# An attention and FFN kernel on one core: the values of pairs 4 to 15 from seven block products in place of eight

## The reference, cut to what matters

```python
D, HEADS, HEAD = 512, 32, 128                  # x is 2 batches x 512 tokens x 512
x = hidden_states
h = layernorm(x)
q = rms_norm(h @ Wq + bq, gq)                  # over all 32*128 columns
k = rms_norm(h @ Wk + bk, gk)
v = h @ Wv + bv
a = softmax(q_head @ k_head.T / sqrt(128))     # per batch and head
o = concat_heads(a @ v_head) @ Wo + bo
x = x + layernorm(o)
x = x + layernorm(ffn(layernorm(x)))           # 512x512 base, 8 gated experts of rank 16
```

## Time and profile before

| | |
|---|---|
| time, median of 3 runs | 1073.78 us (1073.11 to 1077.03) |
| profiled execution, first to last instruction (span) | 1069.7 us |
| the profiled execution's own time | not listed apart; the median of the runs lies 4.1 us above the span |
| TensorE busy | 1052.9 us (98%) |
| VectorE, ScalarE, GpSimd busy | 789.6 (74%), 741.3 (69%), 681.1 us (64%) |
| TensorE's granted clock, mean | 0.998 of full speed |

### The profile page before, as it was taken

How to read it: one execution, slowest core, us unless ns; L and a number is a source line. 1 busy time by engine, 2 the same in 40 slices (tenths; PEclk the granted TensorE clock), 3 DMA queues, 4 the chain that set the end, 5 groups by cost and what they waited for, 6 DMA issues and landing times.

```text
span 1069.7 us, 20038 instructions
## 1 busy us (share of the span) xinstructions
PE 1052.9 (98%) x5781; PEld 563.7 (53%) x5781; DVE 789.6 (74%) x1831; ACT 741.3 (69%) x1470; POOL 681.1 (64%) x597
## 2 busy tenths in 40 slices
PE   7999999999999999999999999999999999999997
PEld 4444444444445655555555555555555555555454
DVE  8767766666645887777777777777777777778887
ACT  4666766666656787676777767677776767777756
POOL 2667767676657476676666667666666766666713
PEclk9999999999999999999999999999999999999999
DMA  6688985656663679977676776767677676765702
GB/s 240 175 237 261 269 232 194 223 215 222 203 142 135 199 187 267 227 173 177 177 184 165 189 179 165 176 178 187 162 190 179 163 176 180 189 163 128 175 33 79
DMA packets 312072, 197.76 MB, mean 185 GB/s; under 512 B 275424, under 2 KB 279392, under 8 KB 312032
## 3 DMA queue, kind: packets, MB, share of 16 engines
q1 hardware_dynamic: 304400, 193.71, 65.5%
q10 hardware_dynamic: 7632, 3.57, 1.5%
HBM read 94.45 MB, written 35.68 MB: 122 GB/s over the span
## 4 chain that ended last, share of the span: by engine, by line
PE 91%; DVE 5%; ACT 2%; DMA 1%; issue 1%; SPq 0%; POOL 0%; DVEq 0%; ACTq 0%
PE ps L1236 30%; PE ps L1237 30%; PE ps L1238 30%; DMA wa_stage<-w_qk 1%; DVE pair_q L2061 1%; ACT ps L1031 0%; DVE ps L2047 0%; DVE stats L1630 0%; DMA pair_k<-pair_q 0%; ACT xh L1024 0%; ACT pair_q L1040 0%; PE ps L1348 0%; DVE y L2011 0%; DVE wa_lo L1735 0%; DVE y L2172 0%
## 5 line engine op out<-in xcount | busy, mean ns | idle before, releaser
L2047 DVE TENSOR_SCALAR_CACHE_REDUCE ps<-ps,score_down 128x512 f32<-128x512 f32 x256 | 177.5, 756 | 88.6 <-PE ps L1238 87.9
L2061 DVE SCALAR_TENSOR_TENSOR pair_q<-ps,row_inv,pair_q 128x512 f16<-128x512 f32 x256 | 174.5, 744 | 54.7 <-ACT pair_q L1040 54.6
L1031 ACT ACTIVATE ps<-ps,neg_max 128x512 f32<-128x512 f32 x256 | 168.2, 657 | 44.9 <-DVE ps L2047 44.9
L1236 PE MATMUL ps<-xh,wa_hi 128*128 128x512 f16 x512 | 194.3, 379 | 1.8 <-DVE wa_lo L1735 1.8
L1237 PE MATMUL ps<-xl,wa_hi 128*128 128x512 f16 x512 | 194.3, 379 | 0.0
L1238 PE MATMUL ps<-xh,wa_lo 128*128 128x512 f16 x512 | 194.3, 379 | 0.0
L1040 ACT ACTIVATE pair_q<-ps,row_inv 128x512 f16<-128x512 f32 x256 | 154.9, 688 | 21.5 <-DVE row_inv L2054 21.5
L758 POOL CAST oth<-o_t 128x512 f16<-128x512 f32 x62 | 37.8, 609 | 201.0 <-ACT o_t L1005 200.9
L664 POOL TENSOR_TENSOR acc<-acc,squares 128x512 f32<-128x512 f32 x120 | 151.1, 1281 | 1.7 <-ACT squares L882 1.7
L1237 PE MATMUL ps<-wv_lo,xh 128*128 128x256 f16 x512 | 139.7, 273 | 0.0
L1236 PE MATMUL ps<-wv_hi,xh 128*128 128x256 f16 x512 | 139.7, 273 | 0.0
(11 more groups left out here) (236 smaller groups left out, 2220.9 us busy)
## 6 DMA issues: line engine op xcount, KB each, us to landing
q_k_scratch<-qk_out SPq DMA_DIRECT2D x64, 512.0 KB, 3.9
qk_in<-q_k_scratch SPq DMA_DIRECT2D x64, 512.0 KB, 3.4
wa_stage<-w_qk SPq DMA_DIRECT2D x32, 512.0 KB, 4.8
u_stage<-w_vo SPq DMA_DIRECT2D x32, 512.0 KB, 5.5
wv_stage<-w_vo SPq DMA_DIRECT2D x16, 512.0 KB, 4.2
wo_stage<-w_vo SPq DMA_DIRECT2D x16, 512.0 KB, 4.4
qk_tops<-qk_top_scratch ACTq DMA_DIRECT2D x27, 128.0 KB, 4.2
y<-x SPq DMA_DIRECT2D x8, 256.0 KB, 5.4
```

Of the source, the lines that this page charges most:

```text
L1031: act.activation(ps[:, SCORE + i, :], ps[:, SCORE + i, :], ACT.Exp, bias=neg_max[:, sl, i:i + 1], scale=-1.0, accum_out=row_sum[:, sl, i:i ...
L1236: pe.matmul(outp, lhs[0], rhs[0], start=first, stop=False)
L2047: dve.tensor_scalar(ps[:, SCORE + i, :], ps[:, SCORE + i, :], score_down[:, sl, i:i + 1], None, ALU.mult, ALU.min, accum_out=neg_max[:, sl ...
L2061: dve.scalar_tensor_tensor(out=pair_q[:, 1, i, :], in0=ps[:, SCORE + i, :], scalar=row_inv[:, sl, i:i + 1], in1=pair_q[:, 0, i, :], op0=AL ...
```

## The change

Values of pairs 0 to 3 are computed as before (those of pair 3 in part into bank OB). For pairs 4 to 15 the kernel takes two pairs together (512 columns of v). With x1 and x2 two tiles of 128 tokens, each cut into two halves of the contraction (256 of 512), and the weights cut likewise by contraction half and by pair, the product is a 2 x 2 by 2 x 2 block product. It is computed from seven products of blocks (C, A, E, B, D, G, F), each six matmuls of 256 columns (two chunks by the three fp16 halves).

- In stage A GpSimd forms the sums and differences of x in fp16 halves (`form_x`, `split_x`: 36 instructions between its other work, into `xs`). X_UP goes from 2^10 to 2^9.
- In stage B, for each block of two pairs, GpSimd scales both weight pieces with two instructions of 1024 columns (`scale_first`), forms five sums (C, B, E, F, G), and computes seven low halves (`low_w`); ScalarE computes seven high halves (`high_w`). The Wv splits of both engines (L952, L687, L689) go away for pairs 4 to 15.
- A group is two token tiles. It is done in two steps. The step that begins it has C and A (12 matmuls) where `values` stood, and E and B (12) between `rows` and `attend`. The step that ends it has D and G (12) where `values` stood, and F (6) between `rows` and `attend`. There are 24 groups, in steps 11 to 58. Steps 11 to 14 also hold a `values` block (of pair 3). Steps 59 to 62 hold neither.
- Both halves of bank VB (WORK and ROOT, 256 columns each) hold partial sums. Within a group ScalarE saves C (`save_c`), copies ROOT to WORK three times (`copy_root`) and evacuates twice (`high_second`); VectorE forms two sums with the saved C (`first_sums`) and two low halves (`low_second`), all with 256 columns; GpSimd splits the two sums (`split_sums`: two instructions of 512 columns).
- SyncE loads both weight pieces of a block in one step (`load_both`). The semaphores that only counted began instructions become one (`begun`).

Its core:

```diff
-        X_UP, W_UP, QK_UP, P_UP = 2.0 ** 10, 2.0 ** 14, 2.0 ** 9, 2.0 ** 14
+        X_UP, W_UP, QK_UP, P_UP = 2.0 ** 9, 2.0 ** 14, 2.0 ** 9, 2.0 ** 14
...
@@ GpSimd
+            def scale_first(b):
+                pool.wait_ge(f_loaded, 32 * b + 32)
+                pool.sem_inc(begun, 1)
+                pool.tensor_scalar(first_w, first_w, v_up[:, :], 1.0, ALU.mult, ALU.mult).then_inc(w_formed, 1)
+                pool.tensor_scalar(second_w, second_w, v_up[:, :], 1.0, ALU.mult, ALU.mult).then_inc(w_formed, 1)
...
+            def building(c, j):
+                def some():
+                    if j == 0:
+                        form_g(c - 1)
+                    if j == 1:
+                        low_w(c - 1, W_C)
+                        low_w(c - 1, W_A)
...
+                    if j == 5:
+                        scale_first(c)
+                    if j == 6:
+                        form_c_and_b(c)
+                    if j == 7:
+                        form_e_and_f(c)
+                return some
...
@@ ScalarE
-                for i in range(TB):
+                if begins is False:
+                    act.wait_ge(k_low_ready, 2 * gi + 1)
+                    copy_root()
                 for i in range(TB):
                     exponentials(n, sl, i)
+                if begins:
+                    save_c(gi)
                 if prepare:
                     high_k((s + 2) % 4, n + 2)
-                for i in range(TB):
+                if begins:
+                    act.wait_ge(v_copied, 4 * gi + 1)
+                    copy_root()
+                high_halves(n, sl, 0)
+                if begins is False:
+                    act.wait_ge(q_sum_ready, 2 * gi + 2)
+                    copy_root()
+                for i in range(1, TB):
                     high_halves(n, sl, i)
                 if value:
-                    evacuate_v(n + 2, 2 * ((s + 1) % 4), VB)
+                    bank, v = value
+                    evacuate_v(n + 2, 2 * ((s + 1) % 4), bank, v)
+                if part:
+                    high_second(g, gi, slot, not begins)
...
@@ TensorE
+            def product(k, g, half, first):
+                for c in range(2):
+                    x_hi, x_lo = x_operand(k, g, c)
+                    pe.matmul(half, x_hi, w_high(k)[:, c], start=first and c == 0, stop=False, skip_group_check=True)
+                    pe.matmul(half, x_hi, w_low(k)[:, c], start=False, stop=False, skip_group_check=True)
+                    ins = pe.matmul(half, x_lo, w_high(k)[:, c], start=False, stop=c == 1, skip_group_check=True)
+                ins.then_inc(v_part, 1)
+
+            def first_products(begins, g, gi, b):
+                if begins:
...
+                    product(W_C, g, WORK, True)
+                    product(W_A, g, ROOT, False)
+                else:
...
+                    pe.wait_ge(v_copied, 4 * gi + 3)
+                    product(W_D, g, ROOT, False)
+                    product(W_G, g, WORK, False)
+
+            def last_products(begins, g, gi, b):
+                if begins:
...
+                    pe.wait_ge(v_copied, 4 * gi + 2)
+                    product(W_E, g, ROOT, False)
+                    product(W_B, g, WORK, False)
+                else:
...
+                    pe.wait_ge(v_copied, 4 * gi + 4)
+                    product(W_F, g, WORK, False)
+
-            def step(p, s, par):
+            def step(p, s, par, value=None, part=None, b=None, v=(vh, vl), ready=None):
                 n = 4 * p + s
                 pe.wait_ge(qk_lo_ready, n + 1)
                 scores(n, s)
-                values(p, s, par, n)
+                if part:
+                    first_products(*part[0:3], b)
+                if value is not None:
+                    if value == OB:
+                        pe.wait_ge(o_t_ready, n - 1)
+                    values(p, s, par, n, value)
                 rows(p, s, par, n)
-                attend(n - 1, (s - 1) % 2, (s - 1) % 4 // 2)
+                if part:
+                    last_products(*part[0:3], b)
+                if value == OB:
+                    pe.wait_ge(vl_ready, n + 2)
+                if ready:
+                    pe.wait_ge(*ready)
+                attend(n - 1, (s - 1) % 2, (s - 1) % 4 // 2, v=v)
...
@@ VectorE
+            def first_sums(gi):
+                dve.wait_ge(v_part, PARTS * gi + 6)
...
+                for k, half in enumerate((WORK, ROOT)):
+                    dve.scalar_tensor_tensor(out=v_s[:, k, :], in0=half, scalar=V_DOWN, in1=c_s[:, :],
+                                             op0=ALU.mult, op1=ALU.add).then_inc(q_sum_ready, 1)
...
                 inverses(n, sl)
+                if begins is False:
+                    first_sums(gi)
                 for i in range(TB):
                     low_halves(n, sl, i)
                 if value:
-                    split_v(n + 2, 2 * ((s + 1) % 4), VB)
+                    bank, v = value
+                    split_v(n + 2, 2 * ((s + 1) % 4), bank, v)
+                if part:
+                    low_second(g, gi, slot, not begins)
```

More of the change, by code:

```diff
@@ L543, in load_wo, with load_both, step @@
                     "a p (h n) -> p (a h) n", h=2)).then_inc(wo_loaded, 16)
-            def step(p, s, first=False, weights=True, more=True):
+            def load_both(b):
+                for k, part in enumerate((first_w, second_w)):
+                    sp.dma_start(part, w_vo[bass.ds(2 * b + 4 + k, 1)].rearrange(
+                        "a p (h n) -> p (a h) n", h=2)).then_inc(f_loaded, 16)
+            def step(p, s, first=False, weights=False, more=True):
                 n = 4 * p + s
@@ L764, in step @@
+            def step(p, s, par, prepare=True, weights=True, values=False, part=None, early=None, late=None):
                 n = 4 * p + s
                 split_o((s - 2) % 4, n - 2)
+                if early:
+                    early()
                 if prepare:
@@ L793, in _ @@
             last_low_q(3)
-            step(1, 0, 1)
-            for s in range(1, 4):
-                step(1, s, 1)
-            with pool.Fori(1, PAIRS // 2 - 1) as i:
-                for s in range(4):
-                    step(2 * i, s, 0)
-                for s in range(4):
-                    step(2 * i + 1, s, 1)
-            for s in range(4):
-                step(PAIRS - 2, s, 0)
+            for s in range(4):
+                step(1, s, 1, values=True, late=building(0, 4 + s))
+            for j in range(8):
+                step(2 + j // 4, j % 4, j // 4, values=j < 4, part=formed(1, 1, j) if j > 2 else None,
+                     early=last_low_w(1) if j == 4 else None, late=building(1, j))
+            with pool.Fori(1, FORMED // 2) as i:
+                two_pairs(2 * i, 0)
+                two_pairs(2 * i + 1, 1)
+            two_pairs(FORMED, 0, last=True)
+            for s in range(4):
+                step(PAIRS - 2, s, 0, part=formed(FORMED + 1, 1, s) if s < 3 else None)
             step(PAIRS - 1, 0, 1)
@@ L1045, in output, with save_c, copy_root, high_second @@
                 evacuate_o(2 * p + s % 2 - (0 if s >= 2 else 2), (s - 2) % 4, 4 * p + s - 2)
-            def step(p, s, par, weights, value=True, prepare=True, between=None):
+            def save_c(gi):
+                act.wait_ge(v_part, PARTS * gi + 2)
+                act.activation(c_s[:, :], WORK, ACT.Copy, scale=V_DOWN).then_inc(v_copied, 1)
+            def copy_root():
+                act.activation(WORK, ROOT, ACT.Copy).then_inc(v_copied, 1)
+            def high_second(g, gi, slot, last):
+                tile = first_tile(g) + 2 * last
+                act.wait_ge(v_part, PARTS * gi + (7 if last else 4))
+                act.activation(second_values(slot)[0][:, tile, :], WORK, ACT.Copy,
+                               scale=V_DOWN).then_inc(k_high_ready, 1)
+            def high_w(b, k):
+                act.activation(w_high(k).rearrange("p c n -> p (c n)"), w_source(k),
+                               ACT.Copy).then_inc(w_high_ready, 1)
+            def step(p, s, par, weights, value=None, prepare=True, between=None, part=None, build=None):
                 n = 4 * p + s
                 sl = s % 2
+                begins, g, gi, slot = part or (None, None, None, None)
                 output(p, s)
@@ L1195, in norm_ffn @@
                                scale=rstd[:, 3, t:t + 1]).then_inc(ffn_normed, 1)
[L1198 removed]
+            step(PAIRS - 1, 3, 1, nothing, prepare=False, between=high_others)
             for t in range(TB):
@@ L2116, in _ @@
             scores_down(3, 1, 1, 1)
-            step(0, 3, 0, rows=False)
+            step(0, 3, 0, plain, rows=False)
             dve.wait_ge(y_down_ready, 1)
```

482 lines of the change are left out of this document (360 added, 122 removed).

## The result

The changed kernel took 1098.67 us (median of 4 runs, 1097.93 to 1101.51), the kernel before 1073.44 (4 runs): 1.0234 of it, 95% interval 1.021 to 1.0257, so 25.2 us slower, where 17.7 us were forecast. The profiled execution of the changed kernel is the slowest of its four: 1101.51 us, span 1099.7, against a span of 1069.7 before, a difference of 30.0 that the following reading has to place.

A forecast was written before the change was run, and what follows sets the result against it. TensorE's own instruction list was taken to bound the kernel (busy 98%). Terms -15.7 + 19.8 + 8.1 + 0.7 + 1.5 + 3 + 0.3 sum to +17.7 on 1073.8: 1091.5 us, forecast 1080 to 1099 (60%), range 1077 to 1107.

The forecast's parts named there:

- Matmuls, -15.7: TensorE in stage B: 144 fewer matmuls of 256 columns, 0.109 us each, -15.7 us.
- The wait for y, +19.8: First `rows` matmul, steps 15 to 58: TensorE waits 0.45 us a step for VectorE's addition to y, +19.8 us.
- Steps 11 to 14, +0.7: Their `attend` waits 0.35 us for VectorE's low half of v where a group ends, twice, +0.7 us.
- Steps 59 to 62, +8.1: Steps without values or products: most of the 24 dropped matmuls' time not gained, +8.1 us, bounds 0 and 10.
- The copies in bank VB, 0: Copies and sums in VB are done before E and F want them, with 1.0 and 0.3 us to spare: 0.
- GpSimd, +1.5: Stage B: GpSimd's low half of the attention output late in step 6 and four later places, +1.5 us, bounds 0 and 6.
- Short VectorE instructions beside GpSimd, +3: Computing the next step's scale is held by GpSimd's split or sum, delaying maxima: 10 x 0.3 = +3 us.
- Stage A, 0 with a bound of 5: The 36 instructions forming x, 47 us of work for an engine 64% busy, cost nothing; upper bound 5 us.
- y doesn't bind: Rival, first `rows` matmul, steps 15 to 58: no wait, 19.8 us less; 9% for faster, 7% for no change.
- GpSimd as the bound: Rival, stage B: GpSimd's work stretches by a fifth to 10.7 us and every step waits; 1100 to 1118 us, 6%.
- F's longer chain: Rival, steps that end a group: F waits 0.35 us in 22 steps, perhaps 0.8 in 11; 1100 to 1109 us, 15%.
- TensorE's clock: Rival, over 463 us: clock granted at 0.96 rather than in full, +19 us, 1110 us; 3%.

The follow-up runs named there:

- experiment 1: Also called y_first: changed kernel with VectorE's first addition to y ahead of the four maxima of its step; 1073.86 us, 1.002 of the kernel before.
- experiment 3: Kernel before, with the second half of its values block moved behind rows in steps 4 to 61; 1099.89 us, 1.0262 of the kernel before.
- forms_early: Same run as experiment 4: changed kernel with GpSimd's forms of x ended two rounds earlier in stage A; 1092.38 us, 1.02 of the kernel before.
- experiment 8: Also called single_scale: changed kernel with one scalar operation, not two, in GpSimd's scalings of weights; 1103.42 us, 1.026 of the kernel before.
- experiment 4: Same run as forms_early: changed kernel with GpSimd's 36 instructions forming x ended two rounds earlier in stage A; 1092.38 us, 1.02 of the kernel before.
- both_fixes: Also called experiment 5: changed kernel with y's first addition ahead of the maxima and forms of x two rounds earlier; 1068.76 us, 0.9963.
- experiment 10: both_fixes with the loop over steps 16 to 47 written out straight on four engines; 1067.61 us, 0.9935 of the kernel before.
- experiment 7: Also called pool_more: both_fixes with GpSimd's low half of k computed twice in every step; 1070.13 us, 0.9978 of the kernel before.
- experiment 9: Kernel before, with a second scalar operation (times 1.0) in GpSimd's scalings of weights; 1073.38 us, 0.9997 of the kernel before.

## Why the prediction came out as it did

The direction and the main mechanism were right, the size 7.5 us short, inside the range. That steps 15 to 58 came out at 9.6 with 10.2 forecast is in part luck: 4.5 us of the forecast (GpSimd 1.5, short VectorE instructions 3) were not there, and 3.9 that it had not (1.4 more of y, 1.7 of F, 0.8 at the loop's turn) made up for them. By its steps:

*Matmuls, -15.7.* Right: blocks of 6 and 12 part matmuls last 0.65 and 1.31.

*The wait for y, +19.8.* Right, and shown three ways: by the rows of step 22, by taking it out (experiment 1) and by making it alone in the kernel before (experiment 3). By the starts it sums to 21.2 in steps 15 to 58: 0.44 in the steps of the loop, 0.53 in the twelve outside it, where `rows` starts at 4.43 (not explained), 1.1 in step 32, of which 0.7 belong to the loop's turn.

*Steps 11 to 14, +0.7.* 0.45, in step 12 alone.

*Steps 59 to 62, +8.1.* Mis-sized: 11.0 in this profile, 9.4 in that of forms_early. The term that failed is step 60, put at nothing gained and nothing lost. Its `rows` was forecast at t = 5.3 and came at 6.28:

```profile
1007.51 0.59 PE L1555 MATMUL ps<-wo_hi,oth 128*128 128x512 f16 x1 [3.52 <-DVE y L2394]
1007.89 0.63 PE L1556 MATMUL ps<-wo_lo,oth 128*128 128x512 f16 x1
```

The row_inv of step 59 was held by GpSimd (1.07 us at 996.70), the factors came behind it, and behind the stand TensorE went on at half its clock (starts 0.38 and then 0.43 apart), which I had priced for the loop but not for single stalls. The two can be told apart. The clock is 1.6 of it, and it does not always come: in forms_early the same stand left the clock full, and the step is 11.45 us long and not 13.07:

```profile
997.28 0.38 PE L1561 MATMUL ps<-wo_hi,oth 128*128 128x512 f16 x1 [3.52 <-DVE y L2400]
997.50 0.38 PE L1562 MATMUL ps<-wo_lo,oth 128*128 128x512 f16 x1
```

The held row_inv is 1.0 of it, and comes from the edit of the diff that I had passed over, the second scalar operation: with the old scalings (experiment 8) row_inv takes 0.17 there, `rows` starts at 5.29 (forecast 5.3) and the step lasts 10.47 (10.39).

*The copies in bank VB, 0.* Nearly: ScalarE's takes 0.38 (0.43 estimated), VectorE's sums 0.41 (0.48). F is late by some 1.7 us over 44 steps, 1.3 of it in steps 24, 40, 48 and 56, where row_inv is held; with the old scalings of experiment 8 it isn't late there.

*GpSimd, +1.5.* Not there: TensorE waited for its otl nowhere in the loop. The term took 1.57 and 3.1 us for the scalings; the edit of the diff that I had passed over made them 0.69 and 1.12. With the durations that I assumed, such a lateness appears, in four places and larger than the 0.2 each that I had allowed (experiment 8).

*Short VectorE instructions beside GpSimd, +3.* The locks are there, the cost is not. In the changed kernel:

```profile
693.01 1.15 DVE L2336 TENSOR_SCALAR score_down<-rms,exp_scale 128x5 f32<-128x5 f32 x1
...
694.59 0.76 DVE L2436 TENSOR_SCALAR_CACHE_REDUCE ps<-ps,score_down 128x512 f32<-128x512 f32 x1 [0.43 <-PE ps L1557]
```

score_down took 0.85 to 1.16 in seven places, and here ended 0.43 before the maxima could begin, with the sum of GpSimd beside it (692.86 to 694.13), which the forecast had put later. row_inv took 1.07 to 1.17 in 23 steps, and cost something only where F or step 60's maxima stood behind it. With the old scalings it does so in two (experiment 8).

*Stage A, 0 with a bound of 5.* **The step that failed:** 7.1. That is what the stand for the sum and all else ahead of step 0 cost in this profile; the stand itself and the clock behind it are 6.1. The argument was an average, 47 us of work for an engine busy 64%, in a stage in which TensorE never waits for it. But the last forms stood directly ahead of GpSimd's last squares, and TensorE's next work hangs on their sum. The kernel before had 0.17 us of room there, which its timeline of GpSimd showed and I didn't read:

```profile
340.37 1.27 POOL L710 TENSOR_TENSOR acc<-acc,squares 128x512 f32<-128x512 f32 x1 [0.17 <-ACT squares L882]
```

Experiments 4 and 5 show it: with the forms two rounds earlier the wait is gone.

*Unforecast:* the turn of a loop twice as long as before, 1.5 us here (0.8 in step 31, 0.7 within the 21.2 above), 2.0 in both_fixes (experiment 10).

*The rivals.* That y doesn't bind fell by experiments 1 and 3. GpSimd as the bound fell by experiment 7. F's longer chain showed only once y was out of its way. TensorE's clock stayed at full level (1.00) through the changed kernel's loop, which had 2.5 us idle in 84; ahead of the last 3 us it fell to half only behind the three single stands of 2.86, 2.54 and 3.52 us, all outside the loop. So the kernel that the Trainium skill tells of (TensorE: Matmul & The Clock Gate, A second HAM failure mode), whose short idles made the clock oscillate, is not this one.

## What to carry to other kernels

Work taken from the bounding engine is gained only if what it covered still arrives in time: list, for each block that shrinks, what the next block waits for and when that ends, and move it in its own queue in the same edit. Here one line on VectorE turned 2.3% slower into 0.2% slower, and a better place for side work on GpSimd turned that into a gain of 0.4%. A shorter instruction is a move as well: what stands behind it starts earlier, and may then run beside something that it holds. Room on an engine is a matter of places, not of its busy share: look at what stands directly ahead of each result that the bounding engine waits for. And price a wait by starts against starts; the idle time of a pipelined engine is too small.

## What the hardware showed that was not expected

- GpSimd's TENSOR_SCALAR on 128x512 f32 takes 1.563 us with one scalar operation and 0.692 with two, on 128x1024 2.842 and 1.12. Both directions were tried (experiments 8 and 9). Why is not shown.
- A stall can cost more than its length, and not in every execution. The profiles of the changed kernel and its seven variants have twelve stands of TensorE of 2.3 to 3.5 us ahead of the FFN. Behind eight of them it went on at 1.2 of its 2.4 GHz for a while (matmuls of 512 columns some 0.43 apart from 349.33 to 351.85, then 0.22), which cost 1.6 us in step 60 and 3.1 at the end of stage A. Behind four it kept the full clock: 2.38 (y_first), 2.42 (pool_more), 2.54 (single_scale) and 3.52 (forms_early). The length of the stand does not decide it.
- A short VectorE instruction beside GpSimd's TENSOR_TENSOR takes as long as that does (row_inv 1.16 and not 0.17 us, experiment 9). So a faster GpSimd can make VectorE slower: VectorE's busy time rose from 789.6 to 838.2 us by GpSimd's shorter scalings.
- In both_fixes the single turn of a loop of 16 steps (163 us) stopped VectorE for 2.94 us and TensorE for 0.69 with no wait named but issue. The kernel before goes six times through a loop of 8 steps and shows none of it: each of those steps is 10.39 us long, with VectorE's maxima at their place. That the body's length is the cause was not tried, only that the turn is.
